# A decoder layer on one core: the last block's second norm computed beside block 0 instead of block 6, y's norm on other places, the loop written out

## The reference

```python
mod = (silu(c) @ wmod).reshape(1, 6, 1, 512)          # sa, ca, ga, sb, cb, gb
h = layernorm(x) * (1 + ca) + sa
x = x + ga * attn(h)                                  # the mixer: linear attention and SwiGLU
h = layernorm(x) * (1 + cb) + sb                      # the second norm
gate_up = h @ w_gu.T                                  # 4-bit weights, one scale per 128 inputs
y = (silu(gate) * up) @ w_down.T
x = x + gb * y / sqrt(mean(y * y) + 1e-6)
```

## Time and profile before

| | |
|---|---|
| median of 3 runs | 1954.58 us (1954.21 to 1956.61) |
| profiled execution | 1954.04 us, its span 1952.2 us, mean granted clock 0.993 |
| PE busy | 1869.9 us, 96% |
| DVE busy | 1406.3 us, 72% |
| ACT busy | 926.1 us, 47% |
| POOL busy | 914.3 us, 47% |
| DMA | 61 GB/s mean |

### The profile page before, as it was taken

One profiled execution on the slowest core, in us unless ns is written; L12 is line 12 of the kernel. 1 busy time (PEld: TensorE's weight loads), 2 busy tenths in 40 slices (PEclk: granted clock), 3 DMA queues, 4 the chain that ended last, 5 costly groups with the idle time before them and its releaser, 6 DMA issues. The chain is left out here.

```text
span 1952.2 us, 25495 instructions
## 1 busy us (share of the span) xinstructions
PE 1869.9 (96%) x8382; PEld 828.0 (42%) x8382; DVE 1406.3 (72%) x1785; ACT 926.1 (47%) x1415; POOL 914.3 (47%) x644
## 2 busy tenths in 40 slices
PE   6988999999999999999999999999999999999796
PEld 2433444444444444444444444443444444444342
DVE  6979768777868876877686785645567766776865
ACT  6753444235235334423523521222676676676573
POOL 2655435234224423523431331312677878778574
PEclk9999999999999999999999999999999999999998
DMA  8312221120211112022020120323101011001011
GB/s 307 129 55 65 76 70 47 51 72 12 86 39 45 54 36 69 21 76 65 18 81 21 36 77 22 95 89 130 64 22 65 1 66 66 32 33 44 0 44 65
DMA packets 71137, 119.38 MB, mean 61 GB/s; under 512 B 5008, under 2 KB 32656, under 8 KB 69648
## 3 DMA queue, kind: packets, MB, share of 16 engines
q1 hardware_dynamic: 71056, 118.40, 18.3%
HBM read 80.11 MB, written 38.27 MB: 61 GB/s over the span
## 5 line engine op out<-in xcount | busy, mean ns | idle before, releaser
L733 PE MATMUL bank<-Y,wsw 128*128 128x512 f16 x3072 | 688.8, 380 | 23.6 <-ACT late L939 14.4
L1140 POOL TENSOR_TENSOR late<-late 128x512 f16<-128x512 f32 x128 | 182.9, 1429 | 622.0 <-ACT late L947 621.2
L733 PEld LDWEIGHTS bank<-Y,wsw 128*128 128x128 f16 x3072 | 299.2, 98 | 396.2 <-ACT late L939 17.8
L2122 DVE SCALAR_TENSOR_TENSOR f_A<-bank,gu_s,f_A 128x512 f32<-128x512 f32 x352 | 260.2, 742 | 171.7 <-ACT f_A L1941 164.4
L708 PE MATMUL bank<-late,wout 128*128 128x512 f16 x1536 | 352.4, 379 | 0.4 <-POOL late L1140 0.4
L2016 POOL TENSOR_TENSOR f_A<-f_A 128x512 f32<-128x512 f32 x176 | 260.1, 1478 | 128.0 <-DVE f_A L2122 128.0
L1941 ACT ACTIVATE f_A<-bank,gu_s 128x512 f32<-128x512 f32 x338 | 231.6, 686 | 159.9 <-PE bank L1873 143.6
L1832 PE MATMUL bank<-f_HH,f_down_hi 128*128 128x512 f16 x704 | 267.6, 382 | 10.0 <-POOL f_HH L2033 9.9
L1206 DVE TENSOR_TENSOR late<-late,bank 128x512 f32<-128x512 f32 x128 | 87.5, 683 | 201.3 <-PE bank L733 192.2
L708 PEld LDWEIGHTS bank<-late,wout 128*128 128x128 f16 x1536 | 150.1, 98 | 188.8 <-issue 12.8
L939 ACT ACTIVATE late<-bank 128x512 f32<-128x512 f32 x128 | 76.4, 597 | 322.2 <-PE bank L733 277.3
(11 more groups left out here) (219 smaller groups left out, 2148.7 us busy)
## 6 DMA issues: line engine op xcount, KB each, us to landing
X<-xT SPq DMA_DIRECT2D x14, 1024.0 KB, 5.5
room<-packed SPq DMA_DIRECT2D x48, 176.0 KB, 2.5
h_scratch<-X SPq DMA_DIRECT2D x8, 1024.0 KB, 4.4
f_X<-x_scratch SPq DMA_DIRECT2D x8, 1024.0 KB, 5.6
x_scratch<-X SPq DMA_DIRECT2D x28, 256.0 KB, 2.2
h_scratch<-SQ SPq DMA_DIRECT2D x28, 256.0 KB, 2.2
outT<-f_X SPq DMA_DIRECT2D x7, 1024.0 KB, 4.2
room<-wswT SPq DMA_DIRECT2D x4, 1024.0 KB, 6.5
```

Of the source, the lines that this page charges most:

```text
L733: mm = nc.tensor.matmul(out[:], wsw[:, pw, k, col:col + P], Y[:, px, k, :], start=(k == 0 and pw == 0 and px == 0), stop=(k == DT - 1 and ...
L1140: nc.gpsimd.tensor_tensor(UG[:, j % 2, 1, :], G, UG[:, j % 2, 0, :], ALU.subtract).then_inc(UG_low, 1)
L2122: nc.vector.scalar_tensor_tensor(a, EV[ev_bank(j, m, steps)][:], gu_s[:, which * I_T + j, g:g + 1], a, ALU.mult, ALU.add).then_inc(by_dve, 1)
```

## The change

1. The second norm of block 7 is computed beside block 0. Its sum and its centring read K directly instead of a copy from DRAM. The mean is made at place 16, the variance at place 30; the banks go round three in steps 4 to 7 of block 0. The two halves are written to a new buffer HS, stored to `h2_dram`, and loaded as any other block's H before block 7.
2. `mixer_result` moves from places 1, 3, 5, 7 to places 6, 7, 8, 9.
3. On ACT the high half of a step (`high`) is issued ahead of the root: place 23 in blocks 1 to 7 (y's), place 31 in block 0 (the variance's). The variance is first copied out of its bank (`keep_var`).
4. y's norm (`norm_y`) is issued at places 29, 32, 33 and 36 instead of 30, 31, 32 and 34.
5. The loop over blocks 2 to 5 is written out; `iteration(...)` becomes the body of a Python loop.

```diff
-        def r_steps(prev, nxt):
-            return range(2, 6) if nxt else range(5, 6) if prev else range(0)
+        def r_steps(b):
+            return range(4, 8) if first(b) else range(5, 6)
...
-        def blocks(eng, iteration):
-            iteration(0, 0, False, False)
-            iteration(1, 1, True, False)
-            with eng.Fori(2, NB - 2, 2) as b:
-                iteration(b, 0, True, False)
-                iteration(b + 1, 1, True, False)
-            iteration(NB - 2, 0, True, True)
-            iteration(NB - 1, 1, True, False)
-        ADD_X, MEAN, CENTRE, SQUARE_N, ADD_N, VARIANCE = 1, 8, 9, 13, 15, 23
-        ROOTS = 24
-        INVERT_N, SCALE_N, HIGH_N, LOW_N = 25, 29, 31, 33
+        MIXER_RESULT = {6: 0, 7: 1, 8: 2, 9: 3}
+        ADD_X, MEAN, CENTRE, SQUARE_N, ADD_N, VARIANCE = 8, 16, 17, 19, 22, 30
+        ROOT = 31
+        INVERT_N, SCALE_N, HIGH_N, LOW_N = 32, 36, 38, 40
...
-        NORM_Y = {30: 0, 31: 1, 32: 2, 34: 3}
+        NORM_Y = {29: 0, 32: 1, 33: 2, 36: 3}
         RESULT = {31: 0, 35: 1, 39: 2, 43: 3}
         OPENS = [(Y_MEAN // DT, 4), (Y_MEAN // DT, 6)]
+        OPENS_FIRST = [(VARIANCE // DT, 4), (VARIANCE // DT, 6)]
...
-            sp.wait_ge(last_stored, 16)
-            sp.dma_start(N[:], x1_t[:, :, tok(NB - 1)]).then_inc(n_loaded, 16)
+            for b in range(1, NB):
+                if b < NB - 1:
+                    load_H(b + 1, (b + 1) % 2)
+                if b == 1:
+                    sp.wait_ge(HS_high, DT)
+                    sp.wait_ge(HS_low, DT)
+                    sp.dma_start(h2_dram[:, NB - 1], HS[:]).then_inc(HS_stored, 16)
+                store(b - 1)
+                load_res(b)
...
+            def keep_var():
+                act.wait_ge(var_red, 1)
+                nc.scalar.activation(RV[:], R[:], ACT.Copy).then_inc(var_kept, 1)
             def var_sqrt():
-                act.wait_ge(var_red, 1)
-                nc.scalar.activation(RV[:], R[:], ACT.Sqrt, bias=eps[:, 0:1]).then_inc(var_root, 1)
+                act.wait_ge(var_kept, 1)
+                nc.scalar.activation(RV[:], RV[:], ACT.Sqrt, bias=eps[:, 0:1]).then_inc(var_root, 1)
...
                         if m == GROUPS - 2:
                             if j:
                                 high(b, j - 1)
-                            elif prev:
+                            elif not first(b):
                                 high(b - 1, I_T - 1)
+                        if first(b) and place == ROOT:
+                            var_sqrt()
+                        if not first(b) and place == Y_ROOT:
+                            y_sqrt(b - 1)
                         if not by_vector(b, j, m):
                             take(b, j, m, steps)
```

More of the change, by code:

```diff
@@ L1836, in down @@
                     mm.then_inc(down_used, 1)
[L1838 to L1844, removed]
+            for b in range(NB):
+                s, steps = b % 2, r_steps(b)
+                if not first(b):
+                    pe.wait_ge(H_loaded[s], 16 * ((b + 1) // 2))
                 for j in range(I_T):
@@ L1847, in iteration @@
                         place = DT * j + m // 2
[L1848 removed]
+                        if m % 2 == 0 and first(b) and place == MEAN:
                             sums_left(b, steps)
[L1850 to L1853, removed]
+                            mean()
+                        if m % 2 == 0 and first(b) and place == VARIANCE:
+                            variance()
+                        if m % 2 == 0 and not first(b) and place == Y_MEAN:
                             sums_left(b, steps)
[L1855 removed]
+                            y_square(b - 1)
                         last = before(j, m, steps)
                         if last is None:
[L1858 to L1860 removed]
+                            pe.wait_ge(*((var_kept, 1) if first(b) else (y_kept, b)))
                         elif not (j == 0 and last[0] and first(b)):
@@ L1951, in silu, with beside_first, beside @@
                 nc.scalar.activation(A[:, slot(j), 0, :], A[:, slot(j), 0, :], ACT.Silu).then_inc(gate_silu, 1)
-            def beside(b, s, place, prev, nxt):
-                if prev and place in COPY_Y:
+            def beside_first(place):
+                due, c = now(place, SQUARE_N)
+                if due:
+                    square_n(c)
+                due, c = now(place, HIGH_N)
+                if due:
+                    split(c)
+                if place == VARIANCE:
+                    keep_var()
+            def beside(b, place):
+                if place in COPY_Y:
                     copy_y(b - 1, COPY_Y[place])
[L1956 to L1959, removed]
+                if place in SQUARE_Y:
                     square_y(b - 1, SQUARE_Y[place])
[L1961 to L1964, removed]
+                if place == Y_MEAN:
                     keep_y(b - 1)
[L1966 to L1972, removed]
+            for b in range(NB):
+                steps = r_steps(b)
                 for j in range(I_T):
                     for m in range(0, GROUPS, 2):
-                        beside(b, s, DT * j + m // 2, prev, nxt)
+                        place = DT * j + m // 2
+                        if first(b):
+                            beside_first(place)
+                        else:
+                            beside(b, place)
                         if m == GROUPS - 2:
@@ L2034, in low, with beside_first, beside @@
                                         ALU.subtract).then_inc(HH_low, 1)
[L2036 to L2043, removed]
+            def beside_first(place):
+                due, n = now(place, ADD_X, 2)
+                if due and n < NSUM:
+                    add_x(n)
+                due, n = now(place, ADD_N, 2)
+                if due and n < NSUM:
+                    add_n(n)
+            def beside(b, place):
+                if place in ADD_Y:
                     add_y(b - 1, ADD_Y[place])
-                if prev and place in RESULT:
+                if place in RESULT:
                     result(b - 1, RESULT[place])
-            def iteration(b, s, prev, nxt):
+            for b in range(NB):
                 for j in range(I_T):
@@ L2055, in iteration @@
                                 low(b, j - 1)
-                            elif prev:
+                            elif not first(b):
                                 low(b - 1, I_T - 1)
-                        beside(b, DT * j + i, prev, nxt)
+                        if first(b):
+                            beside_first(DT * j + i)
+                        else:
+                            beside(b, DT * j + i)
                     half(b, j, 1)
-            blocks(pool, iteration)
             low(NB - 1, I_T - 1)
@@ L2155, in iteration @@
                                 hidden(b, j - 1)
-                            elif prev:
+                            elif not first(b):
                                 hidden(b - 1, I_T - 1)
-            blocks(dve, iteration)
             hidden(NB - 1, I_T - 1)
```

105 lines of the change are left out of this document (48 added, 57 removed).

## The result

The changed kernel took 1943.18 us (median of 4, 1942.68 to 1943.55) beside 1955.59 for the kernel before in the same comparison: 0.9943 of its time, 95% interval 0.9931 to 0.9955. That is 12.4 us faster. I had forecast 25 us, 1929.5 with a range of 1922 to 1941: the direction was right, the size was not, and 1943.18 lies 2 us above the range.

What follows compares the result with a forecast made beforehand. TensorE bounds the kernel, plus places where DVE or the chain ACT to POOL is locally late. -18.6 - 0.9 - 10.5 + 4.9 = -25.1 us from the profiled 1954.04 gives 1928.9, as a median 1929.5; range 1922 to 1941.

Steps and rivals of the forecast that it cites:

- Block 6: Block 6 loses its second norm and becomes like block 2, 87.98 to 69.34: 18.6 us gone; H's load costs nothing.
- The loop: Block 4, first after the back edge, loses its extra 0.9 us without the loop; straight code for blocks 2 to 5 costs 0.
- The edits on y: Blocks 1 to 7: high half ahead of the root and y's norm on other places save 1.5 us each, 10.5 together.
- Block 0: Block 0 takes over the norm, without work on y beside it: +4.9 us, bounds 0 and 12.6.
- the tail: Block 0 from place 32: DVE's reciprocals, scales and low halves exceed TensorE's time at twelve places, +3.2 us.
- the start: Block 0 before the first down projection: multiplications of the mixer's result now come behind the hidden product, -1.3 us.
- the mean: Block 0, place 16: TensorE waits for DVE's take of place 15 and makes the sum, +1.7 us.
- the squares on ACT: Block 0, places 19 to 22: squares on ACT beside a take, with three banks only, +0.4 us.
- Rival 3: The norm costs in block 0 the 18.6 us it cost in block 6: 1943.2 us in all; chance 0.08.
- Rival 2: Blocks 1 to 7: y's edits bring nothing, something else is late and DVE's lag only moves: 1940.0 us; chance 0.15.
- Rival 1: Blocks 1 to 7: the norm at place 29 still costs 1.41 us, giving back 4.9: 1934.4 us; chance 0.12.
- The rival on the slow side: Norm multiplications at 32, 33 and 36 each meet POOL, lasting 1.75 us; block 0 at upper bound: 1965.2 us; chance 0.05.

## Why the prediction was wrong, step by step

- **Block 6, -18.6.** Right: 87.98 to 69.30 is 18.7, and the load of H and the store of HS cost nothing that shows.
- **The loop, -0.9.** The row was right, the term too large: -0.2 over the four blocks. I had the straight code's 0.16 a block in my bounds (block 1's 69.50) and took zero.
- **The edits on y, -10.5.** The step that failed. From 69.49 to 69.29 is 0.2 a block, 1.4 in seven, and not 1.5 a block. I stepped DVE through its takes, and the takes do come in time; the norm's duration at place 29, 0.74, was right too. What I left out is POOL's queue: I asked what stands behind each DVE instruction, and not whether the input of the hidden product was there, nor what the product would last beside POOL's next sum (1.68, not 0.68). This cost 0.88 at place 36, and 0.87 of it came back with the residual addition moved. Even without it the two edits are worth only 69.49 - 68.42 = 1.07 a block: I had let 0.25 of the 0.85 come back at place 26 (measured 0.30), but 0.13, 0.17 and 0.17 more are lost at places 28, 32 and 36. The wait of the hidden product was within reach in the trace of the kernel before, block 2, on DVE and on POOL:

```profile
1544.52 0.68 DVE L2129 TENSOR_TENSOR f_A<-f_A 128x512 f32<-128x512 f32 x1
```
```profile
1542.69 1.71 POOL L2016 TENSOR_TENSOR f_A<-f_A 128x512 f32<-128x512 f32 x1
1544.67 1.65 POOL L2016 TENSOR_TENSOR f_A<-f_A 128x512 f32<-128x512 f32 x1 [0.27 <-DVE f_A L2122]
```

That product started 0.12 us after POOL's half sum had ended at 1544.40; DVE's own lag just covered it. Moving the residual confirmed that this was the next limit.
- **Block 0, +4.9 with the tail.** Measured +6.5 in block 0 and, against ordinary blocks of their own kernels (69.49 written out, 69.29), +1.4 in block 1: +7.9. By terms: the start -1.1 (said -1.3); the mean +1.7 (+1.7); the variance +0.9 (+0.9); the squares on ACT nothing (+0.4); the tail 2.0 in block 0 and 1.4 at place 0 of block 1, +3.4 (+3.2). Missing altogether: 1.0 at each of places 12, 24 and 28, +3.0, where an addition of the norm stands on POOL ahead of the low half. Again POOL's queue, which I had not walked. (In the tail, the place with a reciprocal was counted at 1.6; by the terms given it is 0.94 + 0.66 + 0.17 - 0.08 = 1.69, which makes the tail 3.5 instead of 3.2.)
- **Sum.** -18.6 - 0.2 - 1.4 + 7.9 = -12.3, beside 12.4 by the medians. From the start of block 0 on, the two profiles differ by 12.2 us; as wholes only by 10.8, since the mixer of the profiled execution took 1.4 longer, less than the 3 by which two profiles of the kernel before differ. In the sum of the losses before, 0.85 and 0.95 make 1.8 and not 2.0; the rest is 0.07 at place 8 and 0.14 at place 20.
- **The rivals on the fast side.** Rival 3's 1943.2 is the measured time, by chance: it had the norm cost 18.6 in block 0 and y's edits gain 10.5, and the runs show 7.9 and 1.4. Rival 2 is right in its number for y's edits, close to 0, but its reason holds elsewhere: in block 2 the low half waits for ACT (1.30 us), not for a sum, and it is in block 0 that low halves stand behind a sum on POOL. Rival 1 falls: the norm at place 29 took 0.74 and not 1.41.
- **The rival on the slow side** needed DVE's norms to meet POOL. That mechanism exists (the residual at 33 with the old norm places: 69.72). In the change one norm of a block lasts so long, the last (1.66 us from 1557.12 in block 2), and TensorE loses nothing behind it.

## What to carry to other kernels

When a stall is taken away on a chain that runs over several engines, walk the whole chain again with the new times on every engine's queue, the helper engine's too, and look for instructions whose inputs had only just been in time. On an in-order queue, try a short instruction without haste (a residual, a sum of a mean) behind the link of the chain: here exchanging neighbours gave about 0.87 us in each of seven blocks and 2.7 us in block 0. It isn't free everywhere: with y's norm at its old places the same exchange cost 0.63 a block. So measure edits on one chain in combination, since their gains don't add; those at different stretches did.

## What the runs showed that I had not expected

- The hidden product, 0.68 us alone, takes 1.67 to 1.68 when a POOL instruction has just begun. It began 0.15 us ahead of POOL's sum and took 0.68 (1544.52 and 1544.67, the kernel before), and 0.13 or 0.15 behind and took 1.68 or 1.67 (the change; the residual at 33 with the old norm places). In the first case it was POOL's sum that was longer, 1.65 instead of 1.26. So a move on POOL changes durations on DVE as well as start times. The Trainium skill (SBUF — State Buffer, Who interferes with whom) says that a VectorE instruction with two SBUF inputs contends with a GpSimd instruction that reads SBUF, and that issue order decides which of them is blocked. The 1.68 and the 1.65 here agree.
- The straight code isn't free beside the loop here: 0.16 us in each block of 69.3, of it 0.07 each at places 20 and 32 by the starts of the matmuls. Why stays open.
- The mixer's length moves by 3 us between executions of one kernel (1355.5 and 1358.7), as much as or more than several edits here are worth; block lengths tell them apart.
